# Values of a decoder layer's cross-attention computed with the keys stationary, on one Trainium2 core

## What is computed

```
x = layernorm(x + softmax((x Wq + bq)(x Wk + bk)^T / 8) (x Wv + bv) Wo + bo)       one head of 128
x = layernorm(x + concat_h(softmax(x W_Q[h] (ctx W_K[h])^T / 8) ctx W_V[h]) W_O)  16 heads of 64, 77 keys
x = layernorm(x + experts(x))       8 experts, each takes its 1024 best of 4096 tokens; 128 -> 512 gelu -> 128
```

## Time and profile before

| | |
|---|---|
| median of 3 runs | 668.06 us |
| the profiled execution, its own time | 665.35 us |
| its span, first to last instruction | 663.4 us |
| first cross scores of step 0 start at | 41.47 us |
| first cross scores of step 15 start at | 397.05 us |
| last router matmuls of attention start at | 421.22 us |

### The profile page before, as it was taken

The page is one execution under the profiler, slowest core; times in us unless marked ns, Lnnn a source line. Parts: engine busy times, 40 slices in busy tenths (PEclk is TensorE's granted clock), DMA queues, the critical chain, the costliest instruction groups (busy, mean ns, idle before and its releaser), DMA issues.

```text
span 663.4 us, 11726 instructions
## 1 busy us (share of the span) xinstructions
PE 555.7 (84%) x3846; PEld 464.2 (70%) x3846; DVE 430.6 (65%) x1007; ACT 317.1 (48%) x721; POOL 275.6 (42%) x313
## 2 busy tenths in 40 slices
PE   9989999999999999999999979501399999897700
PEld 9868989989988988988988868301277775465600
DVE  3256766766775785685676667588855687424576
ACT  3655855765765675675676632100133334332215
POOL 7203233322322322332232233000677777777756
PEclk9999999999999999999999989655599999979765
DMA  5011220320221122023042100670123355534662
GB/s 187 27 41 39 97 76 14 96 87 10 86 87 51 45 87 89 8 87 96 0 150 72 55 17 9 227 170 0 42 57 109 125 181 176 171 109 142 217 230 111
DMA packets 50547, 61.09 MB, mean 92 GB/s; under 512 B 10578, under 2 KB 36435, under 8 KB 50260
## 3 DMA queue, kind: packets, MB, share of 16 engines
q1 hardware_dynamic: 45984, 52.00, 24.3%
q0 software_dynamic: 4096, 8.66, 4.6%
q10 hardware_dynamic: 436, 0.03, 0.0%
HBM read 35.37 MB, written 25.30 MB: 91 GB/s over the span
## 4 chain that ended last, share of the span: by engine, by line
PE 46%; DVE 25%; issue 12%; POOL 7%; ACT 6%; DMA 3%; DVEq 0%; POOLq 0%; ACTq 0%
PE PS L1238 10%; PE PS L1477 7%; PE PS L1459 7%; PE PS L1264 6%; PE PS L1246 6%; DVE csum L895 3%; POOL spread L612 3%; DVE above L1013 3%; DVE pc L889 3%; PE PS L1255 2%; DVE cmax L884 2%; POOL shared L602 2%; ACT VOeven L673 2%; DMA shared<-table,idx 2%; DVE shared L945 2%
## 5 line engine op out<-in xcount | busy, mean ns | idle before, releaser
L577 POOL TENSOR_TENSOR pn<-pc,crcp 128x1232 f32<-128x1232 f32 x32 | 72.0, 2250 | 180.2 <-DVE crcp L898 180.2
L602 POOL DMA_INDIRECT shared<-table,idx x64 | 63.1, 986 | 66.2 <-DVE idx L1077 47.3
L1238 PE MATMUL PS<-cT_hi,heads_hi 128*128 128x308 f32 x256 | 83.7, 327 | 1.1 <-DVE shared L945 0.6
L673 ACT ACTIVATE shared<-PS 128x308 f32<-128x308 f32 (+1 forms) x144 | 62.1, 472 | 42.2 <-PE PS L1273 29.8
L1238 PE MATMUL PS<-cT_hi,heads_lo 128*128 128x308 f32 x256 | 78.0, 305 | 0.0
L1238 PE MATMUL PS<-cT_lo,heads_hi 128*128 128x308 f32 x256 | 77.5, 303 | 0.0
L1246 PE MATMUL PS<-shared,x1T 128*128 128x512 f32 (+1 forms) x192 | 72.4, 513 | 4.4 <-DVE pc L889 4.0
L612 POOL DMA_INDIRECT spread<-pn,idx x64 | 66.2, 1034 | 19.8 <-issue 17.7
L808 ACT ACTIVATE shared<-PS,b1T 128x512 f32<-128x512 f32 x64 | 44.0, 687 | 56.0 <-PE PS L1459 56.0
L895 DVE TENSOR_REDUCE csum<-pc 128x16 f32<-128x1232 f32 x32 | 45.8, 1430 | 33.6 <-ACT pc L693 33.6
L1477 PEld LDWEIGHTS PS<-w,shared 128*128 128x128 f32 x512 | 63.8, 204 | 4.1 <-issue 3.8
(11 more groups left out here) (173 smaller groups left out, 1129.1 us busy)
## 6 DMA issues: line engine op xcount, KB each, us to landing
spread<-zeros SPq DMA_DIRECT2D x128, 128.0 KB, 2.1
VOT<-spread SPq DMA_DIRECT2D x64, 256.0 KB, 5.6
xboth<-in_x SPq DMA_DIRECT2D x16, 256.0 KB, 2.7
w<-in_W SPq DMA_DIRECT2D x2, 2048.0 KB, 11.0
table<-x SPq DMA_DIRECT2D x16, 128.0 KB, 1.9
fin<-table SPq DMA_DIRECT2D x1, 2048.0 KB, 20.4
out_x<-fin SPq DMA_DIRECT2D x8, 256.0 KB, 2.0
cin<-in_ctx SPq DMA_DIRECT2D x8, 154.0 KB, 2.6
```

The costliest lines, as they stand in the source:

```text
L577: pool.tensor_tensor(pn[:, e, 0:HK].rearrange("p (h k) -> p h k", h=HEADS), pc[:, e, :].rearrange("p (h k) -> p h k", h=HEADS), crcp[:, e, ...
L602: pool.indirect_dma_start(xg[:, e % 3, h, :], None, table, bass.IndirectOffsetOnAxis(ap=idx[:, e, h:h + 1], axis=0)).then_inc(gathered[e % ...
L673: act.activation(dst, src, ACT.Copy).then_inc(free[bank_of(at, name)], 1)
L1238: i = pe.matmul(bank[:, 0:4 * KEYS], w[a][:, h, :], cT[b][:, :], start=(n == 0), stop=(n == 2))
```

## The change

- The values of a pair are made with the keys stationary. 64 keys (KEYS_MAIN) of each of two batches, copied side by side by POOL into cmain, are the 128 stationary columns; N of four heads, 512 columns, moves. Four units VO0 to VO3 a pair. The result has keys on partitions, and 64-partition halves of it are copied straight into VO, halves that lie elsewhere than in VO changing partitions. No VOT, no transposes.
- The remaining 13 keys of eight batches (104 stationary columns, from an input laid out apart) are made in four units, two in each of two steps of four, copied by ACT to a staging buffer, stored to DRAM by SP in eight small DMAs each half, and loaded into VO's last two blocks by two DMAs a step. pn is laid out to match: POOL divides in two instructions (64 and 13 keys), the blocks are eight of 128 and two of 104.
- The second batch's transposes, output and statistics move to the next step. A is made for four batches over two steps, eight heads each; A has six batch slots. Q, K and V are projected a step sooner. The loop has four bodies and runs three times.
- Self-attention: q is scaled by -1/8 as it is copied, DVE takes the minimum, and this is exp's bias (with scale -1); the scaling instruction goes. The residual is added in PSUM, where statistics and the norm read it.
- DVE's order is another (below), it copies values unit 3 and, in step -1, heads 2, 3, 6, 7 of eight. The fold of Wv and Wo is made with the first part of the set-up.
- `landed` lies behind A's buffer; two memsets go.

The core of the diff:

```diff
-SELF_SCALE = 1.0 / 8.0
+SELF_SCALE = -1.0 / 8.0
+def units_of(phase):
+    units = [(("P2T", 1, g), "post") for g in range(3)]
+    units += [("QK", "project"), (("AV2", 1), "post")]
+    units += [(("VO", u), "values") for u in range(2)]
+    if phase == 3:
+        units += [(("A", h), "A first") for h in range(8)]
+    heads = [(("A", h), "A even" if phase % 2 == 0 else "A odd") for h in early_heads(phase)]
+    units += heads[0:3] + [(("P2T", 0, g), "cross") for g in range(3)]
+    units += heads[3:6] + [("x2T", "post"), (("AV2", 0), "cross")]
+    if phase in (1, 2):
+        units += [(("rest", u), "rest 1" if phase == 1 else "rest 2") for u in range(2 * phase - 2, 2 * phase)]
+    units += heads[6:8] + [("V", "project")] + [(("VO", u), "values") for u in range(2, 4)] + [("LG", "post")]
...
+VALUES_BY_DVE = (3,)
+FIRST_HEADS_BY_DVE = (2, 3, 6, 7)
...
-        FIRST = 4
+        FIRST = 5
+        def halves_of(at, u, copy):
+            to = VO[values_pair(at)]
+            src = ring[bank_of(at, ("VO", u))]
+            rows = slice(KEYS_MAIN * (u // 2), KEYS_MAIN * (u // 2 + 1))
+            for e in range(2):
+                copy(u, src[KEYS_MAIN * e:KEYS_MAIN * (e + 1), :],
+                     to[rows, e, 4 * (u % 2):4 * (u % 2) + 4, :].rearrange("p c d -> p (c d)"), e == 1)
...
SP
+            def store_rest(at, half):
+                for b in range(2 * PHASES):
+                    sp.dma_start(eight[b, 8 * half:8 * half + 8, :, :].rearrange("h k d -> k h d"),
+                                 rows[KEYS_REST * b:KEYS_REST * (b + 1), :, :].rearrange("k u (h d) -> k (u h) d", d=P)
+                                 ).then_inc(rest_out, 16)
...
POOL
+                if runs("post", first):
+                    second_power(p - 1, 1)
                 if cross:
+                    divided(0)
+                if runs("main keys", first):
+                    main_keys()
                 if prep:
                     wait(pool, var1, p + 2)
                     pool.tensor_tensor(rs1[:, :], ve1[:, :], mhalf[:, :], ALU.pow).then_inc(rstd1, 1)
                 if cross:
+                    divided(1)
+                    second_power(p, 0)
...
DVE
+                if cross:
+                    cross_max(0)
+                if prep:
+                    dve.tensor_reduce(smin[:, :], small[:, 0:2 * P].rearrange("p (e k) -> p e k", e=2), AX.X,
+                                      ALU.min).then_inc(smin_done, 1)
+                if cross:
+                    cross_sub(0)
+                if post:
+                    second_stats(p - 1, 1, 1 - parity)
                 if cross:
                     cross_sum(0)
                     cross_max(1)
+                    cross_sub(1)
+                if post:
+                    second_norm(p - 1, 1, 1 - parity, nth - 1)
+                if first == -1:
+                    heads_copy(range(8))
                 if prep:
+                    first_norm()
+                if cross:
+                    cross_sum(1)
                 if prep:
+                        dve.tensor_scalar(x1[1 - parity][:, e, :], small[:, e * P:(e + 1) * P], mv1[:, e, 0:1], rs1[:, e:e + 1],
                 if cross:
+                    second_stats(p, 0, parity)
                     second_norm(p, 0, parity, nth - parity)
+                if first == -1:
+                    heads_copy(early_heads(phase))
+                if runs("values", first):
+                    for u in VALUES_BY_DVE:
+                        halves_of(at, u, copy_half)
...
PE
+                def values(u):
+                    hi, lo = [t[:, values_pair(at), :] for t in cmain]
+                    h = 8 * (u % 2) + u // 2
+                    n_hi, n_lo = [t[:, h:h + 7:2, :] for t in NN]
+                    done(products(unit(name), ((hi, n_hi), (lo, n_hi), (hi, n_lo))), name)
```

More of the change, by code:

```diff
@@ L49, with runs @@
     while len(units) % RING_BANKS:
         units.append((("none", len(units)), None))
+    return units
+def runs(stage, q):
+    if stage == "prep":
+        return -1 <= q < PAIRS - 1
+    if stage == "project":
+        return -2 <= q < PAIRS - 2
+    if stage == "cross":
+        return 0 <= q < PAIRS
+    if stage == "post":
+        return 1 <= q <= PAIRS
+    if stage == "ahead":
+        return q % 2 == 0 and -2 <= q < PAIRS - 2
+    if stage == "main keys":
+        return -2 <= q < PAIRS - 2
+    if stage == "A first":
+        return q == -1
+    if stage == "A even":
+        return q % 2 == 0 and 0 <= q < PAIRS - 2
+    if stage == "A odd":
+        return q % 2 == 1 and -1 <= q < PAIRS - 2
+    if stage == "values":
+        return q == -2 or 0 <= q < PAIRS - 1
+    if stage == "rest first":
+        return q == -2
+    if stage == "rest 1":
+        return q % PHASES == 1 and 1 <= q < PAIRS - 4
+    if stage == "rest 2":
+        return q % PHASES == 2 and -2 <= q < PAIRS - 4
+    return False
@@ L718, in self_pT, with rest_copy @@
                                    ACT.Copy).then_inc(self_free, 1)
-                first = prep and not cross
-                even, odd = ahead and parity == 0, prep and parity == 1
-                heads = even or odd
-                if parity == 0 and prep:
-                    vo_copy(1, 1)
-                if even:
+                def rest_copy(u):
+                    if u == 0 and first > 0:
+                        wait(act, rest_out, 16 * 4 * PHASES * (turn + 1))
+                    if u == 2 and first > 0:
+                        wait(act, rest_out, 16 * 4 * PHASES * (turn + 1) + 16 * 2 * PHASES)
+                    copy(at, ("rest", u), rest_half(at, u), bank(("rest", u))[0:REST, :])
@@ L727, in step @@
+                prep, cross, post = runs("prep", first), runs("cross", first), runs("post", first)
+                values = runs("values", first)
+                heads = runs("A even", first) or runs("A odd", first)
+                if runs("ahead", first):
                     wait(act, c_in, 16 * (nth + 2))
                     act.activation(cT[0][:, :], cin[:, :], ACT.Copy).then_inc(ct_hi, 1)
+                if first == -2 or runs("rest 1", first):
+                    wait(act, cr_in, 16 if first == -2 else 16 * (turn + 2))
+                    act.activation(crest[0][:, :], crin[:, :], ACT.Copy).then_inc(cr_hi, 1)
@@ L761, in step @@
[L761 to L769 removed]
+                for u in range(4):
+                    if runs("rest 1" if u < 2 else "rest 2", first):
+                        rest_copy(u)
+                if heads:
+                    heads_copy(mine[6:8])
@@ L1321, in step @@
                     done(i, "QK")
[L1322 to L1327 removed]
+                if post:
+                    cross_out(1, 1 - parity)
+                if first == -2:
+                    for k in range(FIRST):
+                        setup_wait_copied(pe, k)
@@ new lines, in step @@
+                if runs("values", first):
+                    wait(pe, cmain_done, 1 if first == -2 else p + 2)
+                    values(0)
+                    values(1)
+                if prep and cross:
+                    self_transposes()
+                if cross:
+                    keep_warm(14 if alone else 0)
+                    cross_scores(1)
+                if first == -1:
+                    for k in range(FIRST, len(SETUP)):
+                        setup_wait_copied(pe, k)
+                    self_transposes()
+                    heads(range(8))
@@ L1328, in step @@
+                if prep:
+                    self_values()
+                if runs("A even", first):
+                    wait(pe, ct_lo, nth + 2)
+                if ahead:
+                    heads(mine[0:3])
+                if cross:
+                    keep_warm(6 if alone else 0)
+                    cross_pT(p, 0)
+                if ahead:
+                    heads(mine[3:6])
                 if post:
```

613 lines of the change are left out of this document (327 added, 286 removed).

## The result

The changed kernel took **639.84 us** (median of 4 runs, 638.63 to 643.04) against 668.03 of the kernel before (4 runs, 666.09 to 670.12): a ratio of 0.9585, 95% interval 0.9539 to 0.9631. The forecast was 636, within 626 to 654. The profiled execution took 640.40 against 665.35, 24.95 less, where the sum said 31.7. So the direction and most of the size held, and some 7 us are to be explained.

A forecast was written before the change was run, and what follows sets the result against it. PE bounds the steps until another chain is longer. Steps 1 to 12 -30.5, step 13 -3.8, step 0 -4.3, step 14 -3.0, start +7.1, end +2.8: -31.7 from 665.35 is 633.6, in proportion 636 us; range 626 to 654.

The forecast's parts named there:

- Waits of 0.25 included: Steps 1 to 12 without remaining keys: 20.6 us each, with 0.25 of PE waiting counted in.
- rival (d): Values and remaining keys: 512-column products stream faster, x1 bounds the step at about 19.4, 613 us; chance 0.02.
- PE bounds the steps, and what leaves PE there leaves the time: Steps of the kernel before: PE's work sets their 24.40 and 23.20 us, until a chain through other engines is longer.
- It comes 1.3 later and does not wait: Steps with remaining keys: PE reaches the x1 transposes 1.3 us later and does not wait for x1.
- Off SBUF matters: DVE beside POOL's division: the self maximum's scaling (0.70 us, 0.17 with POOL idle) disappears; the x1 norm stays 0.6.
- I take 0.45 on ACT: Values' half copies between partition halves: 0.45 us each on ACT, 0.6 on DVE.
- rival (c): Values' half copies: changing partitions makes them slower, 680 us at 3.5 us for one; chance 0.03.
- SP costed at nothing: Remaining keys' stores and loads add 1 to 5 us to SP's 5, hidden as SP idles half the step.
- eight units 5.3 ... V 0.5: Start, from the keys at 22.4: eight values units take 5.3 us and V 0.5, clock and ring waits apart.
- so 1.7 are lost here too: Start: PE idles 6.6 us before the values, and the half clock after it loses 1.7 us.
- The moved transposes and output, 3.3 us: Step 15: moved transposes and output, 3.3 us, stand before warming and second scores; the end pays +2.8.
- the rest is as before: End: apart from the moved work, x2's transposes and a short wait, nothing changes up to the last router; +2.8 us.

The follow-up runs named there:

- experiment 1: Kernel before, with VOT's transposes in the loop cut from ten a half to three and the copies kept; 709.70 us (one run).
- experiment 2: Changed kernel with DVE's second sum put ahead of the first norm again; 730.91 us, ratio 1.0282 to the kernel before.
- experiment 3: Changed kernel with the first residual back in SBUF, where statistics and the x1 norm read it; 708.76 us, ratio 0.9963 to the kernel before.
- three_together: Changed kernel with selects behind the keys, all first heads copied by ACT and two last-step warmings dropped; 673.02 us, ratio 0.9456 to the kernel before.
- second_unit_by_dve: As three_together, with the first pair's second values unit copied by DVE instead of ACT; 672.82 us, ratio 0.9454 to the kernel before.
- 4: Changed kernel with A made of two of its three products, the keys' low half left out; 682.50 us (one run).
- experiment 7: Changed kernel with the first eight heads of step -1 all copied by ACT, none by DVE; 681.24 us (one run).
- Experiment 8: Changed kernel without warming ahead of step 15's second scores and the last transposes; 682.61 us, ratio 0.9624 to the kernel before.
- changed_again: Changed kernel, unaltered, as the yardstick on the chip of the combined runs; 683.64 us, ratio 0.9614 to the kernel before.
- keys_first: Changed kernel with POOL's selects moved into step -1, behind its key copies; 676.93 us, ratio 0.9554 to the kernel before.
- no_tail_warming: The same run as Experiment 8: changed kernel without two of the last step's warmings; 682.61 us, ratio 0.9624.
- warm_wait: Changed kernel with 26 warming matmuls on PE between the first projection and its wait for the main keys; 683.24 us (one run).
- sum_before_norm: The same run as experiment 2: changed kernel with the second sum ahead of the first norm; 730.91 us, ratio 1.0282.
- heads_by_act: The same run as experiment 7: changed kernel with step -1's first heads all copied by ACT; 681.24 us (one run).

## Why the prediction was right, and where not

**Steps 1 to 12: right, 254.93 for 255.2, term by term.** The wide product was put at 0.222 and took 0.230; twelve or fifteen of them are 0.1 a step. "Waits of 0.25 included" was right in size: 0.11 before the pn transposes and 0.12 before x1's without remaining keys, 0.14 before pn's with them. "So I add 0.35", the share by which the addition falls short, is what is left: 0.3 and 0.2. The Trainium skill's 131 ns (TensorE: Matmul & The Clock Gate, section Back-to-back issue gap) does not hold for these fp32r products; the trace has 0.230 at full clock, and rival (d) with it falls.

**"PE bounds the steps, and what leaves PE there leaves the time".** Its second half is wrong for the kernel before as far as experiment 1 goes: 0.1 of 1.5 a step, with ACT's copies kept. The forecast did not need it, as the new step was laid out on every engine, but had the change been PE's part alone, this sentence would have promised 2.5 us where a few tenths come.

**"It comes 1.3 later and does not wait"** (x1 in steps with remaining keys): the x1 transposes don't, but the slack is 0.3. What was overlooked is that a bank of the ring is freed by the second residual, queued behind x1 (experiment 2).

**"Off SBUF matters": right.** The scaling of 0.70 is gone, the norm stays at 0.64, and experiment 3 prices it at 1.0 to 1.5 a step. The step argued from the scaling's 0.70 against 0.17; the norm's 2.16 against 0.64 was the larger half.

**POOL and ACT.** Division 2.43 for 2.35, the key copies 0.5 for 0.9. "I take 0.45 on ACT" for a half copy: 0.60 measured, and 0.70 on DVE for 0.6. The row of 1.35 for "three adjacent copies" was misread: two of the three move 512 columns and the last 256. Copies of 512 columns on 128 partitions start 0.49 apart in the changed kernel, the half copies 0.60. It hid behind ACT's slack in the steps, so rival (c) falls, and not in the start.

**SP costed at nothing: right.** No wait for x or for the remaining keys appears in steps 1 to 12.

**Steps 13 and 14: +0.6 and +0.45.** Step 13 was set to the common 20.6; it takes 21.20, with 0.59 of it a wait of a head for the second residual. In step 14 PE waits 1.12 for the division and 0.79 for x1, about what was laid out, and also 0.88 and 0.44 for ACT's pT, with no heads between to cover them.

**The start: +7.1 forecast, +9.6 measured.** The keys came at 22.0 (22.4) and the ring wait was 1.38 (1.3). From the first values to M's set-up the sum has 8.8 (5.3, 1.7, 1.3 and 0.5); it took 10.95, which is 2.15 of the 2.5. Two terms failed. The larger is "eight units 5.3 ... V 0.5": at full clock, in three_together and second_unit_by_dve, this work took 7.17 without its ring wait, 1.4 more. The other is "so 1.7 are lost here too": 10.95 less 1.38 and 7.17 leaves 2.4 for the half clock. That it was 2.4 is chance. The changed kernel's code up to M's set-up was profiled seven times, always with 5.0 to 6.7 of idling, the half clock and a ring wait of 1.38. In four (experiments 3, 4, 7 and 8) the clock was back 3.0 to 3.5 us behind the first values, before the ring wait, and the stretch took 9.68 to 9.70. In the changed kernel, changed_again and experiment 2 it stayed at half for 7.7 to 9.1 us, and the stretch took 10.95 to 11.52. The wait of 2.55 for head 10's copy was foreseen, and experiment 7 prices it at 1.9.

**The tail: +2.8 forecast, +6.4 measured**, the largest miss. Differences of starts in the last step, before and after: first to second scores 5.68 and 9.91, to the first transposes 4.90 and 3.41, to the output 3.38 and 4.62, to the last transposes 2.42 and 4.91, to the router 7.79 and 7.73. "The moved transposes and output, 3.3 us" came to 4.5, as the output waits 0.88 for ACT's pT; 1.5 come back ahead of the first transposes, where PE no longer waits 0.88 for the division and the router is gone, and 1.2 go again ahead of the output, with a wait of 0.88 for x2. The step that failed most is "the rest is as before": it isn't, since the change also adds ten warming matmuls (keep_warm(10 if first == PAIRS ...)) ahead of the last transposes, 2.31 us, and the router's 0.37 moves there. That added line was not counted. Experiment 8, which takes it out with the warming ahead of the second scores, gives 3.0 back, 1.9 of them by this one.

## What to carry to other kernels

Where two engines stand within a few tenths of each other, cutting one of them buys next to nothing (0.1 of 1.5 us here); lay the new step out on all of them, and look for the deadline of each chain, the banks that its last instruction frees included. Code that fills a wait (warming matmuls, constants on an engine with nothing else to do) is priced again whenever the order around it changes: here it cost 3 us at the end and 6 at the start, and moving or dropping it, with the first heads' copies moved to ACT, gave 10.6 us more than the change had. Where a small tile lies is worth a look when DVE reads it while POOL works: PSUM against SBUF was 1.0 to 1.5 us a step. And an experiment that takes work from one engine should take what hangs on it too, or say what it kept: in experiment 1 the copies held PE.

## What the hardware showed that was not expected

- The clock's fall is not a function of the wait in front of it. Behind a wait of 1.93 it was 0.57 in one execution and 1.00 in another of the same code; behind 2.55 it stayed at 1.00 in the changed kernel, keys_first and no_tail_warming and fell to 0.50 in changed_again, warm_wait and sum_before_norm, which cost 1.2 us; behind 1.84 at the end it was 1.00 or 0.60. Behind 5.0 to 6.7 us of idling it was at 0.50, the 1.2 GHz level, each time. What decides in between stays open; no run here isolates it.
- The second of two norms in SBUF took 1.99 us beside POOL's division where the first took 0.26.
- A 64-partition copy of 512 columns took 0.60 on ACT, no less than one of 128 partitions by its own record, and two in a row 1.20, while two of 128 partitions start 0.49 apart.
- Single steps of the same code were now and then up to 1 us longer, and in step 14 the clock did it: it took 20.25 in changed_again and 20.28 in warm_wait, where the clock was at 0.50 for 3.4 us of it, and 19.65 in the changed kernel, where it stayed at 1.00 behind the same waits of 0.44 to 1.13. With the code of the kernel before it took 22.19 and, in experiment 1's execution, 23.14. In heads_by_act and three_together steps 3, 7 and 11 were 0.1 to 0.4 longer at full clock, the first with a wait of 0.3 for the division; the cause of that was not looked for.
- The part behind the last router took 280 to 289 us in the experiments and 242 in the two kernels above, while steps 1 to 12 of the changed kernel agreed to 0.01 us. The traces that were compared for it show waits of up to 12 us there that the list puts down to "remote", for which the trace has no instruction that ended them (131 to 157 us in all, over engines that wait at the same time), and the two traces of 242 us show none. What stood behind them stays open.
